# Taking the low half of W one slot later, paired with the next unit's high half in opposite quadrants of the TensorE array

## The reference, cut to what matters

```python
state = state * exp(g_t)
corr = einsum('bhk,bhkv->bhv', k_t, state)
v_new = (v_t - corr) * b_t
state = state + einsum('bhk,bhv->bhkv', k_t, v_new)
o_t = einsum('bhk,bhkv->bhv', q_t, state)
```

## Time and profile before

| | us |
|---|---|
| median of 3 runs | 1215.83 (1215.57 to 1220.2) |
| the profiled execution | 1210.69 |
| its span, first to last instruction | 1208.9 |
| PE busy / DVE / ACT / POOL | 1140.1 / 808.9 / 701.4 / 511.0 |
| first chain_y to last chain step | 128.4 to 766.6 |
| slots 10 to 31 (chain_y at 139.0 to the one at 622.0) | 483.0 |

### The profile page before, as it was taken

How to read it: one execution, slowest core, us unless ns; L and a number is a source line. 1 busy time by engine, 2 the same in 40 slices (tenths; PEclk the granted TensorE clock), 3 DMA queues, 4 the chain that set the end, 5 groups by cost and what they waited for, 6 DMA issues and landing times.

```text
span 1208.9 us, 30366 instructions
## 1 busy us (share of the span) xinstructions
PE 1140.1 (94%) x12324; PEld 788.2 (65%) x12324; DVE 808.9 (67%) x1444; ACT 701.4 (58%) x1212; POOL 511.0 (42%) x719
## 2 busy tenths in 40 slices
PE   7788899999999999999998999869999999999997
PEld 2444455555555555555555566659989999998976
DVE  4897677868768769679667465566565666665552
ACT  3776466666667676676676766524444444445443
POOL 1659476585675774873876921200010000001000
PEclk9999799999999999999999999889999999999999
DMA  3123233644644544555547322351112222111100
GB/s 119 45 53 80 67 59 59 111 89 72 110 78 70 117 71 73 126 109 116 132 66 186 126 67 68 89 195 45 46 45 51 52 64 56 45 45 48 30 17 9
DMA packets 147274, 93.84 MB, mean 78 GB/s; under 512 B 80672, under 2 KB 130720, under 8 KB 146240
## 3 DMA queue, kind: packets, MB, share of 16 engines
q1 hardware_dynamic: 145984, 91.71, 34.6%
q10 hardware_dynamic: 1152, 0.21, 0.1%
HBM read 54.77 MB, written 14.55 MB: 57 GB/s over the span
## 4 chain that ended last, share of the span: by engine, by line
PE 61%; POOL 14%; DVE 7%; issue 5%; SPq 5%; DMA 5%; ACT 3%; ACTq 0%; POOLq 0%; DVEq 0%
PE proj L478 13%; PE out L1511 5%; PE turned_v_chain L1511 5%; POOL inverse L1219 4%; PE proj L1569 4%; POOL rank_one L1216 4%; PE turned_v_chain L1577 4%; PE proj L1450 4%; DMA o_rs<-o_rs_quarters 3%; PE gram L493 3%; PE gram L1485 2%; DVE conv L1014 2%; PE out L502 2%; SPq L423 1%; PE proj L1499 1%
## 5 line engine op out<-in xcount | busy, mean ns | idle before, releaser
L1014 DVE SCALAR_TENSOR_TENSOR conv<-proj,kq_weights,conv 128x504 f32<-128x504 f32 (+2 forms) x261 | 189.9, 731 | 24.2 <-ACT conv L753 17.5
L478 PE MATMUL proj<-xT,vg_weights 128*128 128x512 f32 x384 | 190.1, 618 | 2.6 <-DMA vg_weights<-in_vg_w 2.5
L1810 POOL TENSOR_TENSOR rope<-rope_part,rope_part 128x512 f32<-128x512 f32 x32 | 40.1, 1273 | 337.8 <-DVE rope_part L1747 337.8
L1014 DVE SCALAR_TENSOR_TENSOR conv<-proj,vg_weights,conv 128x504 f32<-128x504 f32 (+2 forms) x192 | 140.8, 734 | 49.3 <-ACT conv L753 44.2
L478 PE MATMUL proj<-xT,kq_weights 128*128 128x512 f32 x348 | 167.5, 608 | 0.2 <-DVE conv L1014 0.2
L1219 POOL TENSOR_TENSOR inverse<-inverse,rank_one 128x30 f32<-128x30 f32 (+14 forms) x240 | 124.9, 521 | 18.8
L1216 POOL TENSOR_TENSOR rank_one<-inverse 128x30 f32<-128x30 f32 (+14 forms) x240 | 116.9, 487 | 15.8
L478 PEld LDWEIGHTS proj<-xT,vg_weights 128*128 128x128 f32 x384 | 68.2, 192 | 65.8 <-issue 59.3
L478 PEld LDWEIGHTS proj<-xT,kq_weights 128*128 128x128 f32 x348 | 61.0, 191 | 67.0 <-issue 64.4
L493 PEld LDWEIGHTS gram<-keys_q 128*64 128x64 f32 x896 | 57.0, 137 | 54.7 <-ACT keys_q L764 36.3
L1586 ACT ACTIVATE rstd<-rstd 128x1 f32<-128x1 f32 x48 | 9.7, 202 | 140.7 <-DVE rstd L1694 140.7
(11 more groups left out here) (247 smaller groups left out, 2436.1 us busy)
## 6 DMA issues: line engine op xcount, KB each, us to landing
kq_weights<-in_kq_w SPq DMA_DIRECT2D x32, 390.0 KB, 6.4
vg_weights<-in_vg_w SPq DMA_DIRECT2D x32, 390.0 KB, 6.3
o_scratch<-oT SPq DMA_DIRECT2D x32, 256.0 KB, 2.4
o_in<-o_scratch SPq DMA_DIRECT2D x16, 512.0 KB, 4.0
o_rs<-o_rs_quarters SPq DMA_DIRECT2D x88, 64.0 KB, 6.2
diagonal<-gram_decayed SPq DMA_DIRECT2D x128, 32.0 KB, 1.9
inverse<-inverse SPq DMA_DIRECT2D x32, 128.0 KB, 2.8
q_first<-rope SPq DMA_DIRECT2D x128, 32.0 KB, 1.9
```

The lines of the kernel that those rows point to most:

```text
L478: mm = e.matmul(bank(c, u)[:], w[:, (k * 3 + c % 3) * 128:(k * 3 + c % 3 + 1) * 128], xT[g][:, k, :], start=(k == 0), stop=(k == KD - 1))
L1014: e.scalar_tensor_tensor(acc(c, u)[:, :, back:], src[:, :, 0:S - back], weights(c, u)[:, j:j + 1], acc(c, u)[:, :, back:], ALU.mult, ALU.a ...
```

## The change

Where a unit is *joined* (units 0 to 27), the high half goes to the bank of the decays (EB) in partitions 64 to 127, not to CH. In units 0 to 26 the low half is left for the next slot (*low_later*), in which one routine, chain_high_and_low, alternates for each sequence one 64 x 64 product of unit uc (rows and columns 64 to 127 of the array, 32 streamed columns) with one of unit ud (rows and columns 0 to 63, 64 streamed columns). It stands before project K0. So 32 products of 32-column weights become 16 of 64-column weights. ACT copies both results one after the other before K0's first tap, POOL's scaling of W moves behind the first of now three pieces of elimination, chain_y waits for less_sum in place of copy_w_low, the inverse goes out as two DMAs in the turning slot and two in the next one, and after slot 31 output and norm stand later. The first unit's low half leaves the prologue.

```diff
-CUTS = (((1, 1), (1, 5)), ((5, 12), (12, 15)), ((15, 21), (21, 24)), ((24, 31), (31, 31)))
+CUTS = (((1, 1), (1, 1), (1, 5)), ((5, 9), (9, 12), (12, 15)), ((15, 18), (18, 21), (21, 24)), ((24, 28), (28, 31), (31, 31)))
...
+        joined = lambda u: u + LAG < last_slot - 3
+        low_later = lambda u: joined(u + 1)
+        high_chain = EB[:].rearrange("p (b s) -> p b s", b=GB)
...
-                def store_inverse(h):
+                def store_inverse_high(h):
                     e.wait_ge(s_solve, SOLVE * h + TURNED)
                     e.wait_ge(s_zero, 3)
+                    wait(e, s_whi, NS * h)
+                    for j in (2, 3):
+                        e.dma_start(D64[rows(j), :, rows(j % 2)], D32[rows(j), :, :]).then_inc(d_inv, 16)
+
+                def store_inverse_low(h):
                     wait(e, s_wlo, NS * h)
-                    for j in range(NB):
-                        e.dma_start(D64[rows(j), :, rows(j % 2)], D32[rows(j), :, :]).then_inc(d_inv, 16)
+                    for j in (0, 1):
+                        e.dma_start(D64[rows(j), :, rows(j % 2)], D32[rows(j), :, :]).then_inc(d_inv_low, 16)
...
+                    h = solve_at(s, 9)
+                    if h is not None and h > 0:
+                        store_inverse_low(h)
...
                 def decays(u):
                     e.wait_ge(s_steps, u + 1)
                     wait(e, s_ee, u)
+                    wait(e, s_whiout, u - LAG + 1)
...
-                    wait(e, s_wloout, u)
+                    if low_later(u - 1):
+                        wait(e, s_sub, u)
+                    else:
+                        e.wait_ge(s_wloout, u)
...
+                def chain_high_and_low(u, v):
+                    if part(u) == 0:
+                        e.wait_ge(d_inv, 32 * (batch(u) + 1))
+                    e.wait_ge(s_d10out, 2 * (u + 1))
+                    e.wait_ge(s_ee, min(u + LAG, U))
+                    if part(v) == 0:
+                        e.wait_ge(d_inv_low, 32 * (batch(v) + 1))
+                    e.wait_ge(s_sub, v + 1)
+                    for b in range(GB):
+                        hi = e.matmul(high_chain[64:128, b, 32:], D64[64:128, GB * part(u) + b, :],
+                                      M[u % LAG][64:128, b, 32:], start=True, stop=True)
+                        lo = e.matmul(chain[0:64, b, :], D64[0:64, GB * part(v) + b, :],
+                                      M[v % LAG][0:64, b, :], start=True, stop=True)
+                        if b == GB - 1:
+                            hi.then_inc(s_whi, 1)
+                            lo.then_inc(s_wlo, 1)
...
                 def chain_sum_low(u):
                     e.wait_ge(s_whiout, u + 1)
+                    wait(e, s_wloout, u)
...
-                chain_low(0)
...
-                    if s > U:
+                    if s > U and not low_later(ud - 1):
                         norm(ud - 1)
...
+                    if s > U and low_later(ud - 1):
+                        norm(ud - 1)
...
+                    if live(uc) and joined(uc):
+                        chain_high_and_low(uc, ud)
...
-                    if live(uc):
+                    if live(uc) and not joined(uc):
                         chain_high(uc)
...
-                    if live(ud) and not live(ua):
+                    if live(ud) and not live(ua) and not low_later(ud):
                         output(ud)
...
+                        if low_later(ud) and not live(ua):
+                            output(ud)
...
-                        chain_low(uc)
+                        if not low_later(uc):
+                            chain_low(uc)
...
                     if live(ua):
+                        copy_w_high(uc)
+                        copy_w_low(ud)
                         tap(K0, ua)
...
-                    if live(ud):
-                        e.wait_ge(s_wloout, ud + 1)
...
+                    if live(ud):
+                        e.wait_ge(s_wloout, ud + 1)
...
+                    if solving and h > 0:
+                        eliminate(h, CUTS[cut][1])
```

More of the change, by code:

```diff
@@ L586, in chain_high @@
                     if part(u) == 0:
-                        e.wait_ge(d_inv, 16 * NB * (batch(u) + 1))
+                        e.wait_ge(d_inv, 32 * (batch(u) + 1))
                     e.wait_ge(s_d10out, 2 * (u + 1))
+                    out = high_chain if joined(u) else chain
+                    if joined(u):
+                        e.wait_ge(s_ee, min(u + LAG, U))
                     for b in range(GB):
                         for i in (0, 1):
-                            mm = e.matmul(CH[rows(i + 2), b * S + 32:(b + 1) * S], D64[64:128, GB * part(u) + b, rows(i)],
+                            mm = e.matmul(out[rows(i + 2), b, 32:], D64[64:128, GB * part(u) + b, rows(i)],
                                           M[u % LAG][64:128, b, 32:], start=True, stop=True)
                     mm.then_inc(s_whi, 1)
+                def chain_high_and_low(u, v):
+                    if part(u) == 0:
+                        e.wait_ge(d_inv, 32 * (batch(u) + 1))
+                    e.wait_ge(s_d10out, 2 * (u + 1))
+                    e.wait_ge(s_ee, min(u + LAG, U))
+                    if part(v) == 0:
[9 more added lines that the diff above has]
+                            lo.then_inc(s_wlo, 1)
                 def chain_sum_low(u):
                     e.wait_ge(s_whiout, u + 1)
+                    wait(e, s_wloout, u)
                     for b in range(GB):
@@ L603, in chain_low @@
                 def chain_low(u):
+                    if part(u) == 0:
+                        e.wait_ge(d_inv_low, 32 * (batch(u) + 1))
                     e.wait_ge(s_sub, u + 1)
@@ L789, in copy_w_high @@
                         e.wait_ge(s_zero, 3)
-                    e.activation(W[u % 2][64:128, :, 32:], chain[64:128, :, 32:], ACT.Copy).then_inc(s_whiout, 1)
+                    out = high_chain if joined(u) else chain
+                    e.activation(W[u % 2][64:128, :, 32:], out[64:128, :, 32:], ACT.Copy).then_inc(s_whiout, 1)
                 def keys(j, u):
@@ L878, in scalar @@
                 copy_w_high(0)
-                copy_w_low(0)
                 for s in range(LAG + 1, SLOTS):
@@ L944, in scalar @@
                         silu(K0, ua, keys(0, ua))
+                    if live(uc) and not live(ua) and low_later(ud):
+                        silu_gate(uc)
                     if live(ud):
@@ L951, in scalar @@
                     if live(uc):
-                        silu_gate(uc)
-                        copy_w_low(uc)
+                        if live(ua) or not low_later(ud):
+                            silu_gate(uc)
+                        if not low_later(uc):
+                            copy_w_low(uc)
                     if s in rope_slots:
@@ L1325, in gpsimd @@
                             scale_rows()
-                        eliminate(h, CUTS[cut][1])
+                        eliminate(h, CUTS[cut][2])
                     if prepare_at(s) is not None and prepare_at(s)[1] == KRS:
@@ L1335, in delta_phase @@
     tiles["ints"], tiles["scales"] = ints, scales
-    done = {"o": s_og, "scaled": s_gr, "stored": d_out, "weights": d_w, "first": d_first, "uvo": d_uvo, "ffn": s_wgt, "ints": d_ints, "decays": s_ee,
+    done = {"o": s_og, "w_high": s_whiout, "scaled": s_gr, "stored": d_out, "weights": d_w, "first": d_first, "uvo": d_uvo, "ffn": s_wgt, "ints": d_ints, "decays": s_ee,
             "gram": s_gm, "gate": s_silu[G], "v1": s_conv[V1], "high": s_wlo, "low": s_wloout, "solve": s_solve}
@@ L1441, in out @@
                         e.wait_ge(done["decays"], U)
+                        e.wait_ge(done["w_high"], U - NS)
                     elif u == 1:
```

24 lines of the change are left out of this document (13 added, 11 removed).

## The result

The changed kernel takes 1227.94 us in the median of 4 runs (1224.81 to 1229.93), beside 1215.7 for the kernel before: a ratio of 1.0091 with a 95% interval of 1.0058 to 1.0123. Timed once more on another chip it took 1226.92, 1.0108 (1.0084 to 1.0132) of the kernel before there. So it is 12 to 13 us slower; 2.9 us slower was forecast, with 1204 to 1232 as range. The profiled execution took 1229.93 us, with a span of 1228.1 against 1208.9. What follows explains the 19.2 us between two traces, of which 12 to 13 stand in the medians.

The account below looks back on a forecast made before the run. Two loops bound it: PE's, and one of POOL, DVE, SP and back to PE; POOL leads after slot 32. Slots 10 to 31 -1.1, prologue -2.5, slots 32 to 36 +6.5: +2.9, 1218.7 us; own range 1213 to 1226, overall 1204 to 1232.

Parts of the forecast that it names:

- PE's own part: The joined pair on PE takes 1.05 us in place of 1.63, a gain of 0.58 a slot; ends 0.62 and 2.1.
- POOL, k = 15 to 20: Six slots: POOL waits 1.9 us for the low half, squares start at 17.2; gain 0.15 each, -0.9 in all.
- k = 5 to 11: Six slots where POOL has four steps before the wait and nothing is late: 0.4 us gained each, -2.4.
- Prologue: First unit's low half, its ACT copy and two hand-overs leave the prologue: -2.5 us, between -1.4 and -2.7.
- The turning pair: Slot where elimination ends and the next: DVE's turn 1.85 us later, V1 waits about 1.2; +0.45 a pair, +2.2 for five.
- Slots 32 to 36: POOL leads, so every wait of W's scaling counts: 4.2 - 1.5 + 3.8 = +6.5 us at column scaling; bounds 0 and +9.
- from there PE runs on as before: After the column scaling in the last slots, PE was taken to lose nothing beyond the +6.5 us.
- The sum's sign: Whole kernel slower: -1.1 - 2.5 + 6.5 = +2.9 us, to 1218.7 us.
- No wait on POOL: Rival, faster: low half copied before POOL asks, all 22 slots keep 0.4 us; 1203 us; chance 0.22.
- The tail absorbs it: Rival, no change: the pair replaces chain_low in slots 33 to 36, +6.5 becomes 0 to 1; 1213 us; chance 0.18.
- DVE overflows: Rival, slower: a turning pair passes on all of its 1.85 us lateness, +2 a pair; 1227 to 1229 us; chance 0.10.
- The corners don't overlap: Rival: each pair takes 2.1 us on PE, +1.05 in 22 slots; 1240 us; chance 0.08.

Follow-up runs that it names:

- turning cut: Changed kernel with all seven last elimination steps ahead of the scaling of W in slots where the elimination ends, column scaling behind it: 1218.44 us, 1.0028 of before.
- oT first: Changed kernel with POOL scaling oT ahead of W in slot 33 alone: 1224.66 us, 1.0098 of before; again 1223.5 beside the changed kernel's 1226.92.
- POOL's two reorderings: On oT ahead of W: from slot 33 more elimination steps ahead of W's scaling, 1220.69 us; then also k = 21 to 23 and column scaling ahead, 1216.97 us.
- all of POOL's reorderings: Changed kernel with oT ahead of W in slot 33, and from slot 33 elimination steps and slot 36's column scaling ahead of W: 1216.97 us, 1.0029 of before.
- loads later: Changed kernel with SP's large output-weight loads issued one slot later, behind the vg_weights load for slot 35: 1233.34 us, 1.0158 of before.

## Why the prediction was right in sign and short in size

- *PE's own part.* Right. The pair takes 1.08 us where 1.05 was taken from output's rows. A flat price of 60 cycles a matmul, as the Trainium skill has it in TensorEngine Tiling (Array Packing), Performance Considerations, taken for each of the profile's 32 instructions, would by estimate have made it 0.8, and the trace does not agree.
- *POOL, k = 15 to 20.* Right in each row: scaling of W 10.8 us into the slot (10.7), after a wait of 1.86 (1.9), squares at 17.23 (17.2), slot 0.15 shorter (0.15). k = 5 to 11: 0.35 shorter (0.4).
- *Prologue.* -2.65 for -2.5.
- *The turning pair.* The mechanism was right, and its place not. DVE's turn starts 16.62 us in, where 16.59 was worked out. But the work that it pushes back first is the convolution of K1, and PE's product for Q in the same slot waits for that bank (1.48 us); I had looked only at V1 in the slot behind, which does not wait. The turning slot is 1.35 to 1.43 longer and the next 0.4 to 1.1 shorter, so a pair costs 0.2 to 1.0, in all +3.0 for five where +2.2 was forecast. The turning cut shows that the wait in the middle of the elimination is the cause.
- *Slots 32 to 36: the step that failed.* +6.5 with +9 as upper bound; measured +16.2, and +4.1 more in slot 37. The row scaling at 653.6 looks right to 0.2 us (653.46), but that was luck: slot 33 begins at 638.58 in place of 640.79, so that the scaling comes 14.9 us into it where 12.8 were summed. And the pair does not wait for the inverse's DMA, as was assumed; it starts at 649.00 right behind the turn of V, because PE came out of a wait of 3.48 us with V0 at the lower clock (3.78 us) and then waited 0.87 for the root. What was summed, however, was POOL's lateness alone, and it stopped at the column scaling. Three terms were missing. First, "oT 1.27" stood in the sum as time on POOL, without the store behind it on SP and the loads behind that store: 3 to 5 us by the version with oT first. Second, the low half in slots 34 and 35 was priced as in the middle of the kernel, 1.9 us behind POOL's demand, when it hangs on PE, and PE on that load: the wait was 1.44 us in slot 34, but 8.96 in slot 35, the columns came at 707.0 and not near 700, and "from there PE runs on as before" was false, since PE then waited 5.15 us and went on at the lower clock. POOL's two reorderings gave 8.0 us of the last slots back. Third, PE's own order: with the output behind the pair and norm behind V0, nothing covers ACT's copy (1.14) and the root (0.87), which goes with the +1.26 of slot 34, where PE waits for nothing else. What was left after all of POOL's reorderings, 7.7 us over the kernel before, is put down to this, to the extra group that slot 36 has (the pair and chain_low both), to a second norm in slot 37, and to the load (4.02 us of wait in that run); it was read from rows and not tried one by one.
- *The time and the range.* The sum's sign is right. The 1227.94 measured lie outside the forecast's own range (1213 to 1226) and inside 1204 to 1232, which had been widened for rivals; no rival's mechanism brought it there, so that the range held by luck.
- *The rivals.* "No wait on POOL" was wrong in the changed kernel, but the turning cut makes it true where it matters. "The tail absorbs it" was wrong: the last slots are 20 us longer. "DVE overflows" named the time that came, for another reason: no turning pair lost 2 us. "The corners don't overlap" was wrong, and its price for them, 2.1 us a pair, was not far from the 1.80 measured when they are not alternated.

## What to carry to other kernels

A change can pay in the steady part of a pipeline and lose it all where the pipeline runs empty: price the last slots by themselves, with the covers that are gone there, and let the change stop before them if they lead by another engine. When an instruction gets a new wait, follow what is queued behind it through every queue, the DMA issuer's too, up to a wait on the busiest engine, and then ask what clock that engine comes back with. Where a wait is unavoidable, put it behind the work that others need and not in the middle of it: moving three steps ahead of it was worth 1.5 us in each turning slot.

## What the runs showed of the hardware

How far two 64 x 64 corners of the array overlap hangs on the order of issue: the same 16 products (32 instructions) took 1.08 us with neighbouring products in different corners and 1.80 in two blocks. An idle PE costs more than its idle time: after 8.19 us without work, a group of four instructions of 512 columns took 3.78 us and not 1.98, and after 5.15 us chain_low took 1.92 and not 1.08 and the next such group 3.78 again, with a granted clock of 0.50 from 710 to 719. The price did not grow with the gap: after 3.48 us it was 3.78 too, and after 11.44 us (loads later) 3.38.
